# Top-4 routing of a mixture-of-experts layer: maxima marked by replacement, counts summed in PSUM, softplus by two subtractions

## The chip, the cores and the metric

One core of a Trainium2 chip runs the whole program. The metric is the time of one execution on the device in microseconds, the median over the runs shown; lower is better.

## The reference

The input x is 16 batches of 128 rows of 256 numbers. Four layers follow each other, each on the layer norm of x and added back to it: a gated long convolution with a context, a feed-forward layer with low-rank experts (top 2 of 16, softmax of the two), a quantized cross attention of 16 heads, and a feed-forward layer with 32 experts. The change sits in the routing of the last one, with two instructions in that of the second. Cut to it:

```python
logits = flat @ router_w.T                       # 2048 tokens x 32 experts
scores = jnp.sqrt(jax.nn.softplus(logits))
_, idx = jax.lax.top_k(scores + expert_bias, 4)
topv = jnp.take_along_axis(scores, idx, axis=1)
topv = topv / (topv.sum(axis=-1, keepdims=True) + 1e-20)
```

Each token's row then goes through its four experts (two products with a clamped gate, one back) and the results are summed with the weights topv; a shared expert takes all tokens.

## The kernel before

Each engine runs one program, written as a loop over ticks; a table per engine (T_PE, T_DVE, T_ACT, T_POOL, T_SP) says at which tick a step is written out for the first time, and most steps recur every 128 ticks, once per batch. The tables set nothing but the order of the instructions in each engine's queue; each queue is worked off in order, and semaphores tie the queues together. So at any time the steps of the convolution of one batch, the second layer of an earlier one and the attention of one before that are interleaved. From tick LOOP on the expert loop runs: 95 tiles of 128 rows, each with a gather, two transposes (L364, L365), the gate and up product (L380), the clamp and product on VectorE (L695, L697, L702), tanh on ScalarE (L1135), a transpose (L370), the down product (L347) and an indirect store.

Names in the code: PE is TensorE, dve VectorE, act ScalarE, pool GpSimd, sp SyncE. The four PSUM banks `ps` are handed out round robin by `bk.take`; whoever takes a bank waits for the semaphore of its last reader.

Routing works on groups of batches: 0 to 2 have four batches (128 columns of logits side by side), 3 and 4 have two. Group g's steps are: ScalarE takes abs and exp(-|l|) (step "ra", L1291, L1293); VectorE adds 1 ("rb", L945); ScalarE takes Ln ("rc", L1297); VectorE corrects the rounding of 1 + e by multiplying with e/((1+e)-1), adds max(l, 0) ("rd", L949 to L966); ScalarE takes the square root ("re", L1301); VectorE refines the root by one step, adds the bias, takes MAX8 and the maxima's indices ("top", L970 to L989); it builds the 0/1 mask of the four best by comparing a row of expert numbers with each index ("mb", L996 to L1003); PE multiplies the mask with a strict triangle (a token's place among its batch's tokens of this expert, L569) and with ones (the batch's count, L570), "rk"; VectorE adds the counts batch after batch into `cum`, adds place, count and the expert's base address, masks it and takes the four addresses with MAX8 ("cum", L1011 to L1026). GpSimd then scatters the token rows to these addresses in HBM (L1395). Each table load of ScalarE (ACT_TABLE_LOAD) appears under the line that needs it. After group 3 a table of tiles is computed from `cum` (L1028 and on), after group 4 the rest of it (L1030).

Steps that share queues with routing and that the prediction speaks of: L1213 copies the transposed, weighted low-rank values to SBUF, and PE's L469 multiplies with them; L1256 are the four exponentials of a head group, L900 its maxima, L1248 the copy behind which PE's L590 waits; L658 to L664 quantize, and PE's L493 and L514 transpose what they give; L856 adds the second layer's result, L653 and L655 take the statistics for the next norm, which GpSimd finishes (L1311 to L1315); L529 transposes the last norm's rows and takes the bank behind the counts; L839 computes 1 + or - tanh for the first router's two weights.

## Time and profile before

| | |
|---|---|
| median of 3 runs | 732.0 us (728.5 to 733.68) |
| the profiled execution | 729.9 us, its span 728.1 us |
| PE busy | 598.3 us, 82%, 4047 instructions |
| VectorE busy | 483.3 us, 66%, 1497 instructions |
| ScalarE busy | 379.2 us, 52%, 1106 instructions |
| GpSimd busy | 376.2 us, 52%, 526 instructions |
| granted TensorE clock, mean | 0.917 |

Busy time is the sum of an engine's instructions; the rest of the span it waits. The clock is given as a share of 2.4 GHz; 0.5 is the lower of its two levels. In lists in order of time a bracket behind an instruction gives the idle time of its engine just before it and the instruction that ended it.

### The profile page before, as it was taken

The page shows a single profiled execution, that of the slowest core. Times are in us where ns is not written, and L with a number is a line of the kernel's source. Part 1 is how long each engine was busy: PE and PEld are TensorE (multiplying, and loading weights), DVE is VectorE, ACT ScalarE, POOL GpSimd, SP SyncE. Part 2 cuts the span into 40 slices and gives each one's busy share as a digit, 9 for nine tenths or more (in the row PEclk, how much of TensorE's full clock was granted, in tenths as well). Part 3 has the DMA queues.
Part 4 walks back from the last instruction along what each step waited for, and adds up shares of the span by engine and source line. Part 5 has one row for each costly group of instructions (what it writes and reads, how often), then busy time and mean ns, then how long its engine had stood idle before and what let it go on. Part 6 is the DMA issues. An engine that isn't in the chain of part 4 may idle for free.

```text
span 728.1 us, 14326 instructions
## 1 busy us (share of the span) xinstructions
PE 598.3 (82%) x4047; PEld 478.0 (66%) x4047; DVE 483.3 (66%) x1497; ACT 379.2 (52%) x1106; POOL 376.2 (52%) x526
## 2 busy tenths in 40 slices
PE   1588899999988899978998897766777999999930
PEld 1477787777876787766876575543556877777810
DVE  1646757867888577767565774483754777655587
ACT  1002556666766367736466945551533666566620
POOL 6767846473563465775434235232163555555560
PEclk9999999999999899989996878895799999999985
DMA  7989999999999962132237925763343555455689
GB/s 275 221 245 335 335 335 334 333 319 324 312 325 312 322 213 84 46 111 75 83 101 266 372 60 161 265 200 114 100 131 95 161 161 155 147 161 158 193 277 302
DMA packets 135740, 155.02 MB, mean 213 GB/s; under 512 B 15248, under 2 KB 124944, under 8 KB 135408
## 3 DMA queue, kind: packets, MB, share of 16 engines
q1 hardware_dynamic: 117536, 122.50, 56.0%
q0 software_dynamic: 7632, 20.98, 8.1%
q10 hardware_dynamic: 10496, 10.62, 4.6%
q8 instruction: 36, 0.59, 0.3%
q14 instruction: 40, 0.33, 0.2%
HBM read 53.92 MB, written 100.28 MB: 212 GB/s over the span
## 4 chain that ended last, share of the span: by engine, by line
PE 61%; DVE 18%; issue 6%; POOL 6%; ACT 4%; DMA 3%; another core or an unknown queue 2%; ACTq 0%; SPq 0%; DVEq 0%; POOLq 0%
PE pc L639 10%; PE ps L380 10%; PE pS L347 6%; PE pS L619 4%; POOL arena L1381 3%; PE ps L605 3%; PE ps L425 2%; DMA work<-y_rows 2%; PE po L590 2%; PE ps L478 2%; PE ps L555 2%; PE ps L465 2%; PE ps L452 2%; PE ps L469 2%
## 5 line engine op out<-in xcount | busy, mean ns | idle before, releaser
L639 PE MATMUL pc<-arena,tk 128*128 128x128 f32 x768 | 112.9, 302 | 14.0 <-POOL arena L1381 7.3
L639 PEld LDWEIGHTS pc<-arena,tk 128*128 128x128 f32 x768 | 101.1, 209 | 27.0 <-issue 14.6
L380 PE MATMUL ps<-arena,work 128*128 x380 | 102.5, 394 | 2.3 <-ACT work L1145 2.3
L1381 POOL TENSOR_TENSOR arena<-arena 128x512 f32<-128x512 f32 x64 | 90.3, 1428 | 18.2 <-ACT arena L1191 18.0
L1395 POOL DMA_INDIRECT expert_rows<-stage,ixl x64 | 63.7, 995 | 44.4 <-DVE ixl L1026 26.0
L1256 ACT ACTIVATE work<-pS,work 128x128 f32<-128x128 f32 x256 | 72.8, 371 | 13.0 <-DVE work L900 11.4
L380 PEld LDWEIGHTS ps<-arena,work 128*128 128x128 f32 x380 | 67.1, 197 | 8.7 <-issue 2.9
L695 DVE TENSOR_SCALAR work<-ps 128x256 f32<-128x256 f32 x95 | 40.1, 422 | 49.1 <-PE ps L380 44.3
L347 PE MATMUL pS<-arena,tk 128*128 x190 | 60.6, 401 | 9.5 <-ACT tk L1140 8.7
L900 DVE TENSOR_REDUCE work<-pS 128x4 f32<-128x512 f32 x64 | 43.8, 684 | 30.9 <-PE pS L619 30.9
L1135 ACT ACTIVATE tk<-work 128x128 f32<-128x128 f32 x95 | 29.4, 310 | 58.9 <-DVE work L695 54.2
L882 DVE TENSOR_TENSOR arena<-pc,arena 128x512 f32<-128x512 f32 x64 | 43.4, 678 | 23.0 <-PE pc L639 23.0
L1323 POOL DMA_INDIRECT y_rows<-tk,work x38 | 41.5, 1093 | 29.0 <-ACT tk L1150 25.1
L347 PEld LDWEIGHTS pS<-arena,tk 128*128 128x128 f32 x190 | 28.6, 189 | 27.6 <-issue 19.3
L1311 POOL TENSOR_TENSOR stD<-stD,epsc 128x1 f32<-128x1 f32 x16 | 3.0, 190 | 84.4 <-DVE stD L655 84.4
L605 PE MATMUL ps<-pk,work 128*128 128x128 f32 x256 | 41.2, 286 | 5.6 <-ACT work L1241 2.9
L1248 ACT ACTIVATE work<-ps 128x512 f32<-128x512 f32 x64 | 37.8, 590 | 5.2 <-remote 2.2
L619 PE MATMUL pS<-arena,work 32*128 32x256 f32 x256 | 39.1, 425 | 0.2 <-ACT work L1241 0.2
L605 PEld LDWEIGHTS ps<-pk,work 128*128 128x128 f32 x256 | 31.3, 147 | 9.1 <-ACT work L1241 3.2
L1311 POOL TENSOR_TENSOR stB<-stB,epsc 128x1 f32<-128x1 f32 x16 | 3.1, 191 | 60.2 <-DVE stB L655 60.2
L425 PE MATMUL ps<-pk,arena 128*128 128x128 f32 x256 | 33.2, 277 | 0.0
L1140 ACT ACTIVATE tk<-po 128x128 f32<-128x128 f32 x95 | 26.1, 275 | 13.4 <-PE po L370 4.4
(288 smaller groups left out, 1484.2 us busy)
## 6 DMA issues: line engine op xcount, KB each, us to landing
expert_rows<-stage SPq DMA_DIRECT2D x32, 2080.0 KB, 21.5
work<-expert_rows SPq DMA_DIRECT2D x95, 130.0 KB
arena<-in_w SPq DMA_DIRECT2D x8, 1536.0 KB
stage<-xn_rows SPq DMA_DIRECT2D x64, 130.0 KB, 2.1
xn_rows<-xnD ACTq DMA_DIRECT2D x16, 512.0 KB
work<-y_rows SPq DMA_DIRECT2D x16, 512.0 KB, 5.7
tk<-in_tk SPq DMA_DIRECT2D x1, 2048.0 KB, 9.8
out<-xs SPq DMA_DIRECT2D x16, 128.0 KB, 2.7
```

What stands on the lines that cost most here:

```text
L347: i = pe.matmul(p[U * k:U * k + U, 0:256], hT[n % 2][:, U * k:U * k + U], arena[:, 512:][:, bass.ds(e, 256)], start=True, stop=True)
L380: i = pe.matmul(p[U * k:U * k + U, 0:256], xgT[n % 3][:, 128 * c + U * k:128 * c + U * k + U], arena[:, 256 * c:][:, bass.ds(e, 256)], sta ...
L425: i = pe.matmul(pv, zv[:, k, :], ident, is_transpose=True, start=False, stop=(k == 7))
L605: i = pe.transpose(p[:, 128 * k:128 * k + 128], Pt[m % 3][:, 128 * k:128 * k + 128], ident)
L619: i = pe.matmul(p[:, 256 * c:256 * c + 256], qT[b % 3][r, 128 * c:128 * c + 128], kz[b % 3][r, c, :, :].rearrange("p a b -> p (a b)"), sta ...
L639: i = pe.matmul(pv, tk[:, h, 128 * d:128 * d + 128], kvv[:, ci, :, :].rearrange("p b (i h j) -> p (b i) h j", i=8, h=8)[:, :, hl, :], star ...
L882: dve.tensor_tensor(zv, cbanks.place["conv", n][:, :].rearrange("p (k h j) -> p k h j", h=4, j=8), x1, ALU.mult).then_inc(s_z, 1)
L900: dve.tensor_reduce(mx[:, g, :], sbanks.place["S", m][:, :].rearrange("p (k m) -> p k m", k=4), AX.X, ALU.max, negate=True).then_inc(s_mx, 1)
L1256: i = act.activation(Pt[m % 3][:, 128 * k:128 * k + 128], sbanks.place["S", m][:, 128 * k:128 * k + 128], ACT.Exp, bias=mx[:, g, k:k + 1])
L1323: pool.indirect_dma_start(out=Yr, out_offset=bass.IndirectOffsetOnAxis(ap=xg[n % NX][:, 256:257].bitcast(U32), axis=0), in_=y[n % NY], in_ ...
L1381: pool.tensor_tensor(kv[kk % 4][:, c, half, :].rearrange("p (i h j) -> p i h j", h=8, i=8), i0, i1, ALU.mult).then_inc(s_kv, 1)
L1395: pool.indirect_dma_start(out=Xs, out_offset=bass.IndirectOffsetOnAxis(ap=ixl[:, b, k:k + 1], axis=0), in_=stage[:, j % NS, :], in_offset= ...
```

## The change

Softplus: ScalarE computes max(l, 0), 1 + e and Ln(1 + e) in one go (a step "ra" of five activations with a table load; "rb" and "rc" are gone), and VectorE forms A = max(Ln - (((1+e) - 1) - e), 1e-30) + max(l, 0). Mask: the bias is added into `score`, whose row has four columns of a very low value behind the 32; the four best values are copied into `m4`, filled up with that low value, match_replace writes `rest` with them replaced, and the mask is where `score` and `rest` differ. Counts: PE adds the earlier batches' counts of a group into the later batches' columns and sums all of the group's in one block of 32 columns; `ckey` holds the running count plus the base address. The first router's 1 + or - tanh moves to ScalarE. Cut to what matters (12 leading blanks are left out):

```diff
@@ -51,7 +52,7 @@
 LATER = {("top", 0): 45, ("top", 1): 45, ("mb", 0): 75, ("mb", 1): 75, ("rk", 0): 101, ("rk", 1): 101,
          ("cum", 0): 105, ("cum", 1): 105, ("list", 0): 136, ("list", 1): -78,
          ("list", 2): -170, ("st", 2): -110, ("list", 3): -182, ("st", 3): -117}
-LAST = {"ra": 1, "rb": 2, "rc": 3, "rd": 4, "re": 12, "top": 21, "mb": 31, "rk": 41, "cum": 42, "list": 52, "st": 0}
+LAST = {"ra": 1, "rd": 4, "re": 12, "top": 21, "mb": 31, "rk": 41, "cum": 42, "list": 52, "st": 0}
 STRIDE = (18, 24, 8, 8, 10)
 RG = 4
 SD = 32
@@ -566,8 +568,12 @@
         p, free = bk.take(("rk", g), s_cum, g + 1)
         pe.wait_ge(*free)
         pe.wait_ge(s_mb, g + 1)
-        pe.matmul(p[:, 0:w], bef[:, :], mb[:, 0:w], start=True, stop=True)
-        pe.matmul(p[:, 128:128 + w], oneb[:, :], mb[:, 0:w], start=True, stop=True).then_inc(s_rk, 1)
+        pe.matmul(p[:, 0:w], bef[:, :], mb[:, 0:w], start=True, stop=False)
+        for o in range(NE, w, NE):
+            pe.matmul(p[:, o:w], oneb[:, :], mb[:, 0:w - o], start=False, stop=(o + NE == w))
+        for o in range(0, w, NE):
+            i = pe.matmul(p[:, 128:128 + NE], oneb[:, :], mb[:, o:o + NE], start=(o == 0), stop=(o + NE == w))
+        i.then_inc(s_rk, 1)
     for m in (*at(t, T_PE["tabE"], 1, 2), *(2 + m for m in at(t, T_PE["tab"], 1, 2))):
         w = 4 * (NWE, NWL)[m // 2]
         p, free = bk.take(("regs", m), s_regs, m + 1)
@@ -836,8 +842,6 @@
         L, top, e2, s, co, c2 = (lv[:, 0:16], lv[:, 16:24], lv[:, 24:28], lv[:, 28:32], lv[:, 32:48],
                                  lv[:, 48:80].rearrange("p (k e) -> p k e", k=2))
         dve.wait_ge(s_e2, 2 * b + 2)
-        dve.scalar_tensor_tensor(out=s[:, 0:2], in0=R("pm"), scalar=e2[:, 1:2], in1=ones[:, 0:2],
-                                 op0=ALU.mult, op1=ALU.add).then_inc(*own.up())
         dve.wait_ge(*own.now())
         dve.tensor_tensor(c2, c2, s[:, 0:2].unsqueeze(2).broadcast_to((128, 2, 16)), ALU.mult)\
             .then_inc(*own.up())
@@ -939,31 +943,16 @@
         w = NE * (b1 - b0)
         return b0, b1, b1 - b0, tuple(rt[:, n, 0:w] for n in range(4))
 
-    for g in (g for g in range(NG) for _ in at(t, when(T_DVE, "rb", g), 1, 1)):
+    for g in (g for g in range(NG) for _ in at(t, when(T_DVE, "rd", g), 1, 1)):
         b0, b1, nb, (S_, A_, B_, C_) = group(g)
         dve.wait_ge(s_ra, g + 1)
-        dve.tensor_scalar(B_, A_, 1.0, None, ALU.add).then_inc(s_rb, 1)
-    for g in (g for g in range(NG) for _ in at(t, when(T_DVE, "rd", g), 1, 1)):
-        b0, b1, nb, (S_, A_, B_, C_) = group(g)
-        dve.wait_ge(s_rc, g + 1)
-        dve.tensor_scalar(B_, B_, -1.0, None, ALU.add).then_inc(*own.up())
-        dve.wait_ge(*own.now())
-        dve.tensor_scalar(S_, B_, 0.0, None, ALU.is_equal).then_inc(*own.up())
-        dve.tensor_scalar(B_, B_, 1e-30, None, ALU.max).then_inc(*own.up())
-        dve.wait_ge(*own.now())
-        dve.reciprocal(B_, B_).then_inc(*own.up())
-        dve.wait_ge(*own.now())
-        dve.tensor_tensor(C_, C_, B_, ALU.mult).then_inc(*own.up())
-        dve.wait_ge(*own.now())
-        dve.tensor_tensor(C_, C_, S_, ALU.add).then_inc(*own.up())
-        dve.wait_ge(*own.now())
-        dve.tensor_tensor(C_, C_, A_, ALU.mult).then_inc(*own.up())
-        dve.wait_ge(*own.now())
-        L = lg4[:, b0:b1, :].rearrange("p b e -> p (b e)")
-        dve.scalar_tensor_tensor(out=A_, in0=L, scalar=0.0, in1=C_, op0=ALU.max, op1=ALU.add)\
+        dve.scalar_tensor_tensor(out=B_, in0=B_, scalar=-1.0, in1=A_, op0=ALU.add, op1=ALU.subtract)\
             .then_inc(*own.up())
         dve.wait_ge(*own.now())
-        dve.tensor_scalar(A_, A_, 1e-30, None, ALU.max).then_inc(s_rd, 1)
+        dve.tensor_tensor(C_, C_, B_, ALU.subtract).then_inc(*own.up())
+        dve.wait_ge(*own.now())
+        dve.scalar_tensor_tensor(out=A_, in0=C_, scalar=1e-30, in1=S_, op0=ALU.max, op1=ALU.add)\
+            .then_inc(s_rd, 1)
     for g in (g for g in range(NG) for _ in at(t, when(T_DVE, "top", g), 1, 1)):
         b0, b1, nb, (S_, A_, B_, C_) = group(g)
         dve.wait_ge(s_re, g + 1)
@@ -973,51 +962,38 @@
         dve.wait_ge(*own.now())
         dve.tensor_tensor(S_, B_, S_, ALU.add).then_inc(*own.up())
         dve.wait_ge(*own.now())
-        dve.tensor_scalar(S_, S_, 0.5, None, ALU.mult).then_inc(*own.up())
-        dve.wait_ge(*own.now())
-        dve.tensor_tensor(v3(C_), v3(S_), R("eb").unsqueeze(1).broadcast_to((128, nb, NE)),
-                          ALU.add).then_inc(*own.up())
+        if g == 0:
+            dve.wait_ge(s_pconst, 2)
+        dve.scalar_tensor_tensor(out=score[:, 0:nb, 0:NE], in0=v3(S_), scalar=0.5,
+                                 in1=R("eb").unsqueeze(1).broadcast_to((128, nb, NE)), op0=ALU.mult,
+                                 op1=ALU.add).then_inc(*own.up())
         dve.wait_ge(*own.now())
         for b in range(nb):
-            i = dve.max(m8[:, b, :], v3(C_)[:, b, :])
+            i = dve.max(m8[:, b, :], score[:, b, 0:NE])
         i.then_inc(*own.up())
         dve.wait_ge(*own.now())
-        for b in range(nb):
-            i = dve.max_index(i8[:, b, :], m8[:, b, :], v3(C_)[:, b, :])
-        i.then_inc(*own.up())
-        dve.wait_ge(*own.now())
-        dve.tensor_copy(f8[:, 0:nb, :], i8[:, 0:nb, :]).then_inc(*own.up())
+        dve.tensor_copy(m4[:, 0:nb, 0:KT], m8[:, 0:nb, 0:KT]).then_inc(*own.up())
         dve.wait_ge(*own.now())
     for g in (g for g in range(NG) for _ in at(t, when(T_DVE, "mb", g), 1, 1)):
         b0, b1, nb, (S_, A_, B_, C_) = group(g)
-        io = R("iota")[:, 0:NE].unsqueeze(1).broadcast_to((128, nb, NE))
-        for k in range(KT):
-            o = A_ if k == 0 else B_
-            dve.tensor_tensor(v3(o), io, f8[:, 0:nb, k:k + 1].broadcast_to((128, nb, NE)), ALU.is_equal)\
-                .then_inc(*own.up())
-            dve.wait_ge(*own.now())
-            if k:
-                dve.tensor_tensor(A_, A_, B_, ALU.add).then_inc(*own.up())
-                dve.wait_ge(*own.now())
-        dve.tensor_copy(mb[:, 0:NE * nb], A_).then_inc(s_mb, 1)
-        dve.tensor_tensor(Sall[:, b0:b1, :], v3(A_), v3(S_), ALU.mult).then_inc(*own.up())
+        for b in range(nb):
+            i = dve.match_replace(rest[:, b, :], m4[:, b, :], score[:, b, :], GONE)
+        i.then_inc(*own.up())
+        dve.wait_ge(*own.now())
+        dve.tensor_tensor(v3(mb[:, 0:NE * nb]), score[:, 0:nb, 0:NE], rest[:, 0:nb, 0:NE],
+                          ALU.not_equal).then_inc(s_mb, 1)
+        dve.wait_ge(s_mb, g + 1)
+        dve.tensor_tensor(Sall[:, b0:b1, :], v3(mb[:, 0:NE * nb]), v3(S_), ALU.mult)
     for g in (g for g in range(NG) for _ in at(t, when(T_DVE, "cum", g), 1, 1)):
         b0, b1, nb, (S_, A_, B_, C_) = group(g)
         p = place["rk", g]
+        last = R("key") if g == 0 else ckey[:, g - 1, :]
         dve.wait_ge(s_rk, g + 1)
-        if g == 0:
-            dve.wait_ge(s_pconst, 2)
-        for b in range(nb):
-            dve.tensor_tensor(cum[:, b0 + b + 1, :], p[:, 128 + NE * b:128 + NE * b + NE],
-                              cum[:, b0 + b, :], ALU.add).then_inc(*own.up())
-            dve.wait_ge(*own.now())
-        dve.tensor_tensor(v3(B_), p[:, 0:NE * nb].rearrange("p (b e) -> p b e", e=NE), cum[:, b0:b1, :],
-                          ALU.add).then_inc(s_cum, 1)
-        dve.wait_ge(s_cum, g + 1)
-        dve.tensor_tensor(v3(B_), v3(B_), R("key")[:, 0:NE].unsqueeze(1).broadcast_to((128, nb, NE)),
+        dve.tensor_tensor(v3(B_), v3(p[:, 0:NE * nb]), last.unsqueeze(1).broadcast_to((128, nb, NE)),
                           ALU.add).then_inc(*own.up())
-        dve.wait_ge(*own.now())
-        dve.tensor_tensor(Ball[:, b0:b1, :], v3(B_), v3(A_), ALU.mult).then_inc(*own.up())
+        dve.tensor_tensor(ckey[:, g, :], p[:, 128:128 + NE], last, ALU.add).then_inc(s_cum, 1)
+        dve.wait_ge(*own.now())
+        dve.tensor_tensor(Ball[:, b0:b1, :], v3(B_), v3(mb[:, 0:NE * nb]), ALU.mult).then_inc(*own.up())
         dve.wait_ge(*own.now())
         for b in range(b0, b1):
             i = dve.max(key[:, b, :], Ball[:, b, :])
@@ -1025,9 +1001,15 @@
         dve.wait_ge(*own.now())
         dve.tensor_scalar(ixl[:, b0:b1, :], key[:, b0:b1, 0:KT], -1.0, None, ALU.add).then_inc(s_ixl, 1)
     for _ in at(t, T_DVE["eta"], 1, 1):
-        floor_of(cum[:, GROUPS[3][1], :], tiles_[:, 1, :], tiles_[:, 0, :], 1.0 / U, 0.5 * (U - 1) / U)
+        dve.wait_ge(s_cum, 4)
+        dve.tensor_tensor(tiles_[:, 1, :], ckey[:, 3, :], R("key"), ALU.subtract).then_inc(*own.up())
+        dve.wait_ge(*own.now())
+        floor_of(tiles_[:, 1, :], tiles_[:, 1, :], tiles_[:, 0, :], 1.0 / U, 0.5 * (U - 1) / U)
     for _ in at(t, T_DVE["ta"], 1, 1):
-        floor_of(cum[:, NB, :], tiles_[:, 1, :], tiles_[:, 0, :], 1.0 / U, -0.5 * (U - 1) / U)
+        dve.wait_ge(s_cum, 5)
+        dve.tensor_tensor(tiles_[:, 1, :], ckey[:, 4, :], R("key"), ALU.subtract).then_inc(*own.up())
+        dve.wait_ge(*own.now())
+        floor_of(tiles_[:, 1, :], tiles_[:, 1, :], tiles_[:, 0, :], 1.0 / U, -0.5 * (U - 1) / U)
         dve.tensor_tensor(tiles_[:, 1, :], tiles_[:, 1, :], taken[:, :], ALU.subtract).then_inc(*own.up())
     for _ in (*at(t, T_DVE["eta"], 1, 1), *at(t, T_DVE["ta"], 1, 1)):
         scan_step(tiles_[:, 1, :], scan[:, 0, :], 1)
@@ -1203,9 +1185,11 @@
         act.activation(hb[0][:, 1, :], place["h", b][0:64, 0:128], ACT.Tanh, bias=hrb1[:, :],
                        scale=0.5).then_inc(s_eh, 1)
     for b in at(t, T_ACT["e2"], 128, NB):
-        e2 = lg[b % 2][:, 24:28]
+        e2, s = lg[b % 2][:, 24:28], lg[b % 2][:, 28:32]
         act.wait_ge(s_e2, 2 * b + 1)
-        act.activation(e2[:, 1:2], e2[:, 0:1], ACT.Tanh, scale=0.5).then_inc(s_e2, 1)
+        act.activation(e2[:, 1:2], e2[:, 0:1], ACT.Tanh, scale=0.5).then_inc(*own.up())
+        act.wait_ge(*own.now())
+        act.activation(s[:, 0:2], R("pm"), ACT.Copy, bias=1.0, scale=e2[:, 1:2]).then_inc(s_e2, 1)
     for b in at(t, T_ACT["wxT"], 128, NB):
         if b >= 2:
             act.wait_ge(s_wb, b - 1)
@@ -1288,13 +1272,15 @@
         act.wait_ge(s_lg4, b1)
         if g:
             act.wait_ge(s_ixl, g)
+        w = NE * (b1 - b0)
         act.activation(A_, L, ACT.Abs).then_inc(*own.up())
+        act.activation(rt[:, 0, 0:w], L, ACT.Relu)
         act.wait_ge(*own.now())
-        act.activation(A_, A_, ACT.Exp, scale=-1.0).then_inc(s_ra, 1)
-    for g in (g for g in range(NG) for _ in at(t, when(T_ACT, "rc", g), 1, 1)):
-        w = NE * (GROUPS[g][1] - GROUPS[g][0])
-        act.wait_ge(s_rb, g + 1)
-        act.activation(rt[:, 3, 0:w], rt[:, 2, 0:w], ACT.Ln).then_inc(s_rc, 1)
+        act.activation(A_, A_, ACT.Exp, scale=-1.0).then_inc(*own.up())
+        act.wait_ge(*own.now())
+        act.activation(rt[:, 2, 0:w], A_, ACT.Copy, bias=1.0).then_inc(*own.up())
+        act.wait_ge(*own.now())
+        act.activation(rt[:, 3, 0:w], rt[:, 2, 0:w], ACT.Ln).then_inc(s_ra, 1)
     for g in (g for g in range(NG) for _ in at(t, when(T_ACT, "re", g), 1, 1)):
         w = NE * (GROUPS[g][1] - GROUPS[g][0])
         act.wait_ge(s_rd, g + 1)
```

The tables of ticks lose "rb" and "rc"; all else keeps its tick. The instructions move at these places. ScalarE in group 0's batch, before; lg is the logits, rt the routing tiles, L1213 the copy for PE's L469:

```order
L1208 ACTIVATE lg<-lg 128x1
L1256 ACTIVATE work<-pS,work 128x128 x4
L1291 ACTIVATE rt<-lg 128x128
L1293 ACTIVATE rt<-rt 128x128
L1213 ACTIVATE work<-ps 128x256
L1297 ACT_TABLE_LOAD
L1297 ACTIVATE rt<-rt 128x128
L1248 ACTIVATE work<-ps 128x512
```

and now (line numbers are those of the changed kernel; L1197 is the same copy, L1232 the former L1248):

```order
L1190 ACTIVATE lg<-lg 128x1
L1192 ACTIVATE lg<-rows,lg 128x2
L1240 ACTIVATE work<-pS,work 128x128 x4
L1276 ACTIVATE rt<-lg 128x128
L1277 ACTIVATE rt<-lg 128x128
L1279 ACTIVATE rt<-rt 128x128
L1281 ACTIVATE rt<-rt 128x128
L1283 ACT_TABLE_LOAD
L1283 ACTIVATE rt<-rt 128x128
L1197 ACTIVATE work<-ps 128x256
L1232 ACTIVATE work<-ps 128x512
```

The table load and Ln moved ahead of the copy, and two activations came in before them. There are 20 table loads in either program. VectorE behind group 0's maxima, before; f is the indices, mb the mask:

```order
L996 TENSOR_TENSOR rt<-rows,f 128x128 x2
L1000 TENSOR_TENSOR rt<-rt 128x128
L996 TENSOR_TENSOR rt<-rows,f 128x128
L1000 TENSOR_TENSOR rt<-rt 128x128
L996 TENSOR_TENSOR rt<-rows,f 128x128
L1000 TENSOR_TENSOR rt<-rt 128x128
L1002 CAST mb<-rt 128x128
L1003 TENSOR_TENSOR Sall<-rt 128x128
L870 TENSOR_TENSOR work<-ps,rows 128x16x16
```

and now:

```order
L980 MATCH_REPLACE rest<-m,score 128x36 x4
L983 TENSOR_TENSOR mb<-score,rest 128x128
L986 TENSOR_TENSOR Sall<-mb,rt 128x128
L874 TENSOR_TENSOR work<-ps,rows 128x16x16
L904 TENSOR_REDUCE work<-pS 128x4
```

Nine instructions became six, with the same neighbours. PE at group 0's counts, now (before, one product with `bef` and one with `oneb`, 128x128 each, stood in this place):

```order
L480 MATMUL ps<-arena,pk 128x128 x4
L571 MATMUL ps<-mb,bef 128x128
L573 MATMUL ps<-mb,oneb 128x96
L573 MATMUL ps<-mb,oneb 128x64
L573 MATMUL ps<-mb,oneb 128x32
L575 MATMUL ps<-mb,oneb 128x32 x4
L611 MATMUL ps<-pk,work 128x128 x4
```

Six products came in ahead of L611, the former L605.

## Rows read from the trace of the kernel before

**Rows 1.** Busy time by stretch; start:end, length, busy us (instructions) by engine, clock, DMA.

```profile
214.00:240.00 26.00, 19.72 (x143) 14.75 (x142) 22.27 (x73) 13.34 (x35) 10.00 (x20) 0.91 1.00 319
510.00:530.00 20.00, 15.70 (x59) 10.73 (x58) 16.03 (x78) 10.37 (x28) 3.95 (x4) 0.78 0.36 98
560.00:600.00 40.00, 39.78 (x215) 31.66 (x214) 29.75 (x107) 25.80 (x96) 22.31 (x24) 1.00 0.52 153
```

**Rows 2.** Page, part 4: shares of the chain that ended last, by engine.

```profile
PE 61%; DVE 18%; issue 6%; POOL 6%; ACT 4%; DMA 3%; another core or an unknown queue 2%; ACTq 0%; SPq 0%; DVEq 0%; POOLq 0%
```

**Rows 3.** PE in order of time: start, length, instruction, [idle before <- releaser].

```profile
227.91 0.30 PE L493 MATMUL ps<-pk,work 128*128 128x128 f32 x1 [1.34 <-DVE work L664]
...
336.01 0.30 PE L493 MATMUL ps<-pk,work 128*128 128x128 f32 x1 [2.21 <-DVE work L664]
```

**Rows 4.** The same view: PE at the bank wait of groups 0 and 1.

```profile
239.91 0.47 PE L529 MATMUL ps<-pk,xnD 128*128 128x128 f32 x1 [2.97 <-DVE rt L1014]
...
347.33 0.33 PE L529 MATMUL ps<-pk,xnD 128*128 128x128 f32 x1 [1.78 <-DVE rt L1014]
```

**Rows 5.** VectorE by line: names, shapes, count | busy us, mean ns | idle before.

```profile
L839 DVE SCALAR_TENSOR_TENSOR lg<-rows,lg,ones 128x2 f32<-128x2 f32 x16 | 6.9, 433 | 6.7 <-ACT lg L1208 6.6
...
L996 DVE TENSOR_TENSOR rt<-rows,f 128x128 f32<-128x128 f32 (+1 forms) x20 | 6.2, 309 | 0.5
...
L954 DVE RECIPROCAL rt<-rt 128x128 f32<-128x128 f32 (+1 forms) x5 | 4.0, 793 | 0.2
...
L986 DVE FIND_INDEX8 i<-m,rt 128x8 uint32<-128x32 f32 x16 | 2.7, 184 | 0.0
...
L986 DVE MATCH_VALUE_LOAD i<-m,rt 128x8 f32 x16 | 1.2, 78 | 0.2
```

**Rows 6.** Order of time around group 1's softplus: VectorE, GpSimd, PE.

```profile
295.96 0.23 DVE L949 TENSOR_SCALAR rt<-rt 128x128 f32<-128x128 f32 x1
...
299.05 0.42 DVE L856 TENSOR_TENSOR xs<-ps,xs 128x256 f32<-128x256 f32 x1
...
300.23 0.19 POOL L1311 TENSOR_TENSOR stC<-stC,epsc 128x1 f32<-128x1 f32 x1 [2.99 <-DVE stC L655]
...
318.39 0.45 PE L529 MATMUL ps<-pk,xnD 128*128 128x128 f32 x1 [4.00 <-ACT xnD L1128]
```

**Rows 7.** Order of time, group 0's burst behind the maxima: VectorE and GpSimd.

```profile
222.02 0.61 DVE L996 TENSOR_TENSOR rt<-rows,f 128x128 f32<-128x128 f32 x2
...
223.32 0.82 DVE L1000 TENSOR_TENSOR rt<-rt 128x128 f32<-128x128 f32 x1
...
225.65 0.42 DVE L870 TENSOR_TENSOR work<-ps,rows 128x256 f32<-128x256 f32 x1
...
223.05 0.95 POOL L1355 TENSOR_TENSOR arena<-arena 128x256 f32<-128x256 f32 x1
```

**Rows 8.** Instructions of one tile, the counts' second product: ns min/median/max.

```profile
L570 PE MATMUL ps<-mb,oneb x5: 193/219/219, 233.8 to 522.2; 128*128 128x128 bf16 x3, 128*128 128x64 bf16 x2
```

**Rows 9.** Order of time around group 0's Ln: ScalarE, then PE.

```profile
190.35 0.37 ACT L1213 ACTIVATE work<-ps 128x256 f32<-128x256 f32 x1
190.73 1.28 ACT L1297 ACT_TABLE_LOAD   x1
192.03 0.31 ACT L1297 ACTIVATE rt<-rt 128x128 f32<-128x128 f32 x1
...
191.36 1.03 PE L469 MATMUL ps<-pk,work 128*128 128x256 f32 x4
192.87 0.43 PE L590 MATMUL po<-work 128*32 128x128 f32 x8 [0.49 <-ACT work L1248]
```

**Rows 10.** Order of time, VectorE: the last group's first and last step.

```profile
512.68 0.20 DVE L949 TENSOR_SCALAR rt<-rt 128x64 f32<-128x64 f32 x1 [1.37 <-ACT rt L1297]
...
524.40 0.17 DVE L1026 TENSOR_SCALAR ixl<-key 128x8 uint32<-128x8 f32 x1
```

**Rows 11.** Order of time, VectorE: a wait for something unknown ("remote").

```profile
549.53 0.43 DVE L919 TENSOR_SCALAR tk<-ps 128x256 f32<-128x256 f32 x1 [4.63 <-remote]
```

21 lines of the change are left out of this document (12 added, 9 removed).

## The prediction

> **What bounds the kernel now.** I read four views in this order: the busy time by stretch, PE's list in order of time with its waits, the groups of instructions by line, and the chain of waits. The stretches show three kinds of time [rows 1]. From 560 to 600 us the expert loop keeps PE busy for 39.78 of 40.00 us at granted clock 1.00, so nothing that leaves VectorE can shorten it. Around the first group's routing (214 to 240 us) PE is busy for only 19.72 of 26.00 us, at clock 0.91, while VectorE is busy for 22.27: here VectorE is late. From 510 to 530 PE idles 4.3 us at clock 0.78 with the last group's routing in between. The whole chain is 61% PE and 18% VectorE [rows 2]. So a VectorE saving is worth something only where PE waits for the queue in which routing sits: 1.34 us in group 0 and 2.21 us in group 1 before the transposes of line 493 [rows 3], and 2.97 and 1.78 us before line 529, which waits for the PSUM bank that the routing counts hold [rows 4]. Group 2's batch shows no such wait of over 0.4 us.
>
> **The change, part by part.** *Softplus.* VectorE's ten steps (line 945 and lines 949 to 966) become three. In group 1 lines 949 to 966 run from 295.96 to 299.05, 3.1 us [rows 6]; three steps of 0.33 us (line 996's 309 ns [rows 5] and the gap behind it) make 1.0, so 2.1 us go; the reciprocal alone is 793 ns. In group 1 these steps stand ahead of the statistics for which GpSimd waits 2.99 us; GpSimd then works on in its order, and PE waits 4.00 us for what comes out of it by way of ScalarE [rows 6]. The line between (856) needs PE's line 469 too, so of 2.1 us I count 1.6. In group 0 the same saving goes nowhere: VectorE next waits for PE's scores.
>
> *Top four.* FIND_INDEX8 with its MATCH_VALUE_LOAD (184 + 78 ns [rows 5]) goes 16 times and match_replace comes 16 times. The trace of before has no match_replace. Its nearest row is that pair, which I take (0.26 us); the upper end is two two-input steps (0.6 us), 16 x 0.35 = 5.5 us more in all; a gain below the pair is excluded, as the instruction reads more columns (36 against 32) and writes them. The comparisons, additions and the cast (20 + 15 + 5 instructions) become one comparison per group. In group 0 the burst that ended with the product ran from 222.02 to 225.65, 3.63 us [rows 7]; four match_replace, the comparison and the product now make 1.05 + 0.33 + 0.33 = 1.7, so 1.9 go. The burst before it loses the index pairs (1.05) and one fused step (0.33), 1.4. So VectorE is 3.3 us earlier at the quantize steps on which line 493 waits. PE idles 26.00 - 19.72 = 6.28 us in this stretch, 2.97 of them the bank wait; of the other 3.3 I count 3.0. In group 1 I count the whole wait, 2.2.
>
> *The shared port.* Line 1000's step takes 0.82 us instead of 0.29 in the same burst, while a GpSimd multiplication with two inputs runs (223.05 to 224.00) [rows 7]; it is one of the removed ones, and its excess of 0.5 us is inside the 3.63. The Trainium skill ("SBUF — State Buffer", Who interferes with whom) says that a VectorE instruction with two SBUF inputs blocks against a GpSimd instruction that reads SBUF, and one with a single input outside the two-port modes does not. The row agrees for the two-input side, and nothing here shows the other. By that rule match_replace never stalls; without it a burst would save up to 0.5 us less. The sum does not use it.
>
> *Counts.* PE gets three more products with shifted columns and three more with 32 in a group of four. Such a product takes at most 0.19 to 0.22 us by itself [rows 8], and its neighbours overlap: between 6 x 0.05 and 6 x 0.2 us; I take 0.3 for a big group and 0.1 for a small one, 1.1 in all. Other PE work is queued behind, so it counts in full. In return the bank is free after two VectorE reads instead of five: at 0.2 us for a 32-column step (as the FIND_INDEX8 of rows 5) that is 0.6 us earlier at each of the two bank waits, 1.3 with the shorter gaps.
>
> *Softmax of the first router.* Line 839 (433 ns mean, 16 times [rows 5]) moves to ScalarE, behind a wait for its own tanh; queued behind it there are the four exponentials. VectorE loses 6.9 us, but for most of that it then waits for PE; ScalarE gets 16 x 0.4 (a step of 0.31 as in rows 9, and the wait). I count a gain of 1.0, with bounds of -6.4 (all of ScalarE's share on the path) and 3 (half of VectorE's).
>
> *ScalarE's order.* The table load and Ln, which stood behind the copy of line 1213, now stand ahead of it, behind two added steps (0.31 us each as the Ln of rows 9). In group 0 the copy began at 190.35; with two steps (overlapping, 0.55), the load (1.28) and Ln (0.31) ahead of it, it begins at 192.5 and ends at 192.9. PE's line 469 needs the copy and began at 191.36; it will begin at about 193.0. PE waited 0.49 us anyway at 192.87 [rows 9], so the loss is about 1.0 us, and the same in group 1. In group 2 PE comes later than the copy. The loss is 2.0, between 0.9 (only the added steps) and 3.5. In the trace Ln starts 0.02 us behind the end of the table load (190.73 + 1.28 to 192.03) [rows 9]. The Trainium skill ("ScalarE: Activation LUTs", What ACT_TABLE_LOAD costs) adds a drain of some 1.38 us to each load. The trace disagrees, and the measurement decides; by the page the copy would be later by as much again and the two losses 2.8 us larger.
>
> *Last two groups.* In the last, VectorE's routing runs from 512.68 to 524.57 with the first tiles of the expert loop in its gaps [rows 10]. Its steps have half the columns, 0.26 us with the gap by my estimate from the mixed 309 ns; softplus loses six steps, the maximum's burst three, the comparisons five, the counts two: 16 x 0.26 = 4.1 us, and ScalarE gets 0.4 more. The tiles pass through PE at a lower clock in this time and PE's idle time is 4.3 us, so I count 2.0. The group before it, with the same instructions, sits between the last two batches: 2.0. Group 2 gets 0.9, for two waits of under 0.4 us.
>
> *Clock.* The granted clock of 0.91 over 26 us is 2.3 us of lost PE work around group 0 [rows 1], in a stretch where the full level gives way behind PE's waits. The bank wait stays for the most part, so I count 1.2 here and 1.0 in group 1: 2.2.
>
> The gains are 1.6 + 3.0 + 2.2 + 1.3 + 1.0 + 4.0 + 0.9 + 2.2 = 16.2 us, the costs 1.1 + 2.0 = 3.1; 13.1 remain at the places. Between them other queues set the pace: GpSimd's row scatters, and waits of several engines for something unknown (4.63 us at 549.53 [rows 11]). By the chain's shares [rows 2] at most 61 + 18 + 4% of the span passes a shift on; with the GpSimd-bound stretch behind group 1 I take 0.65, between 0.4 and 0.85. That gives 8.5 us. Against the profiled execution's 729.9 us this is 721.4. The median of the runs, 732.0, is 2.1 above it; by it the same gain gives 723.5. I forecast 722.
>
> **The rivals.** *(a) Absorbed.* PE works in order, and the saving on VectorE turns into waits for GpSimd or for PE itself: 35% is passed on and the costs are at their upper ends, 16.2 x 0.35 - 4.5 = 1.2 us, so 730. For it speaks that VectorE is only 18% of the chain; against it the waits of rows 3, which name VectorE. *(b) All comes through,* and the clock stays up at the bursts: 13.1 + 2 = 15 us, so 716. The 22.27 busy us of VectorE in 26 speak for it, the bank wait against it. *(c) ScalarE becomes the link: slower.* What routing adds to ScalarE stands ahead of the exponentials and of the copy that PE waits for: 16 x 0.4 and 3 x 1.5 = 11 us, less the 2 of the last group: 739 to 741. It decides from the point where PE waits over 0.4 us for ScalarE in every batch; now there are 0.49 at one place of a routing batch [rows 9]. ScalarE's 13.34 busy us of 26.00 [rows 1] speak against it. *(d) match_replace is dear:* 5.5 us more, a third of them on the path: 724. *(e)* The waits for something unknown come and go with the programs' lengths, by up to 4.6 us either way; this widens every case.
>
> **How the numbers follow.** Forecast (717 to 727, with (d) in it) 0.46, (a) 0.27, (b) 0.19, (c) 0.08. A measurement of this kernel tells about 1%, 7.3 us, from no change: below 724.7 is faster, above 739.3 slower. Faster: 0.19 from (b), 0.36 from the forecast, 0.03 from (a) by (e), 0.58. Slower: 0.07, nearly all from (c). The rest is the same, 0.35. The range takes in (b) and most of (a), 712 to 732; about 0.1 lies above it and 0.08 below.
>
> **What would show it.** Right: the waits before line 493 (1.34 and 2.21) vanish, the bank waits shrink by 0.6 each, the burst of 3.63 us measures 1.4 to 1.8, and VectorE's busy time falls by about 35 us in all (softplus 11, comparisons 12, line 839 7, counts 4, the fused step 1); line 469 in groups 0 and 1 starts late behind a wait for ScalarE. Wrong: if VectorE's busy time falls so and PE's idle time from 214 to 240 does not, (a) holds; if PE's waits for ScalarE grow by over 5 us in sum, (c); if a match_replace takes over 0.5 us, (d).

## The result, and the profile after

The changed kernel took 707.8 us in the median of 4 runs (702.2 to 710.6), the kernel before 732.5 beside it (4 runs): ratio 0.966, 95% interval 0.962 to 0.971, so 24.8 us less. The forecast was 722, a gain of 10. The profiled run after took 710.6 us (span 708.7), the one before 729.9 (span 728.1); the two traces therefore account for 19.4 of the 24.8 us. The runs were taken in six sets, each with runs of the kernel before beside it, and that kernel stood at 728 to 733 us in three of the sets and at 701 to 703 in the other three (on one chip, number 10, at both), so only ratios and differences within a set are compared, and the ratios leave out the executions that fell in a slower state.

Part 1 and the head of part 4 of the page after (the chain before is [rows 2]):

```profile
PE 585.5 (83%) x4069; PEld 470.2 (66%) x4069; DVE 456.7 (64%) x1392; ACT 384.8 (54%) x1132; POOL 375.4 (53%) x527
...
PE 61%; DVE 15%; issue 8%; POOL 6%; ACT 5%; DMA 3%; another core or an unknown queue 2%; ACTq 0%; SPq 0%; DVEq 0%; POOLq 0%
```

VectorE was busy for 483.3 us before and is for 456.7 now. That is 26.6 us less, not the 35 of the forecast. The lines that the change touches did lose about 34 (softplus 11, mask 12, line 839 7, counts 4), but other steps of VectorE took longer, such as this one of the first router, the second behind the step that moved:

```profile
L845 DVE TENSOR_TENSOR lg<-lg 128x16 f32<-128x16 f32 x16 | 6.4, 397 | 0.5
...
L849 DVE TENSOR_TENSOR lg<-lg 128x16 f32<-128x16 f32 x16 | 8.7, 546 | 0.5
```

The first surprise is PE: 598.3 us busy before, 585.5 now, though it got 22 more products. Busy time times mean granted clock is nearly the same, 598.3 x 0.917 = 548.6 and 585.5 x 0.938 = 549.2, and it lies between 546.6 and 550.4 in all eighteen traces without filler products. So the 12.8 us go with the clock. PE's idle time fell by the other 6.6 of the 19.4 us. Busy time by stretch shows where, with the copy of PE's attention output (line 1263 before, 1247 after) as the milestone of each batch. Before, for the batches around the bursts of group 0, group 1 (two batches) and group 2:

```profile
223.90:255.80 31.90, 26.62 (x187) 21.21 (x186) 21.49 (x64) 14.95 (x42) 11.37 (x22) 0.84 1.01 321
...
302.30:332.20 29.90, 24.60 (x186) 20.46 (x186) 20.56 (x63) 16.59 (x44) 22.85 (x30) 0.89 0.26 81
332.20:361.90 29.70, 25.28 (x188) 20.85 (x188) 19.12 (x61) 13.89 (x40) 14.95 (x23) 0.89 0.29 87
...
407.90:437.50 29.60, 26.14 (x165) 19.29 (x166) 23.92 (x86) 18.37 (x49) 9.41 (x15) 0.83 0.48 169
```

and between the same milestones after:

```profile
224.80:252.20 27.40, 24.20 (x194) 19.89 (x193) 18.61 (x55) 15.14 (x43) 11.23 (x21) 0.94 0.99 315
...
298.60:323.80 25.20, 21.91 (x186) 18.10 (x186) 22.41 (x58) 17.03 (x45) 20.77 (x26) 1.00 0.31 97
323.80:354.70 30.90, 26.66 (x197) 21.40 (x197) 18.14 (x53) 14.24 (x40) 15.20 (x24) 0.83 0.28 82
...
400.70:428.50 27.80, 23.00 (x171) 17.60 (x172) 19.68 (x74) 18.64 (x51) 8.74 (x14) 0.94 0.51 177
```

Group 0's stretch is 4.5 us shorter, 2.4 of them PE's busy time, at clock 0.94 instead of 0.84. Group 1 gains 4.7 in its first batch and gives back 1.2 in the second, where the clock stands lower than before. Such a step back in one batch is within what one program does: in two traces of the changed kernel at the other level (changed_again and changed_third, below) this batch took 28.7 and 25.9 us, at clock 0.88 and 1.00. From 214 to 240 us, where the prediction read 6.28 us of idle time of PE, 3.32 are left.

PE in order of time, the waits of [rows 3, 4] and the last one of [rows 6] as they are now:

```profile
227.13 0.30 PE L495 MATMUL ps<-pk,work 128*128 128x128 f32 x1 [0.77 <-DVE work L670]
...
237.33 0.33 PE L531 MATMUL ps<-pk,xnD 128*128 128x128 f32 x1 [2.00 <-DVE ckey L994]
...
312.61 0.30 PE L531 MATMUL ps<-pk,xnD 128*128 128x128 f32 x1 [1.25 <-ACT xnD L1110]
...
326.05 0.30 PE L495 MATMUL ps<-pk,work 128*128 128x128 f32 x1 [0.66 <-DVE work L670]
...
339.22 0.48 PE L531 MATMUL ps<-pk,xnD 128*128 128x128 f32 x1 [1.88 <-DVE ckey L994]
```

And VectorE's burst of group 0, the answer to [rows 7]:

```profile
223.01 0.08 DVE L980 MATCH_VALUE_LOAD rest<-m,score 128x8 f32 x1
223.08 0.18 DVE L980 MATCH_REPLACE8 rest<-m,score 128x36 f32<-128x36 f32 x1
223.18 0.08 DVE L980 MATCH_VALUE_LOAD rest<-m,score 128x8 f32 x1
...
223.79 0.29 DVE L983 TENSOR_TENSOR mb<-score,rest 128x128 bf16<-128x128 f32 x1
224.11 0.83 DVE L986 TENSOR_TENSOR Sall<-mb,rt 128x128 f32<-128x128 bf16 x1
224.87 0.41 DVE L874 TENSOR_TENSOR work<-ps,rows 128x256 f32<-128x256 f32 x1
```

From the first match_replace to the step behind the burst it is 224.87 - 223.01 = 1.86 us, where it was 3.63. One pair starts 0.17 us behind the other (the load overlaps the search before it).

### The profile page after: what moved, and what is told of

The parts are those of the page before. It is cut to its first block, busy times and chain, and to the rows that moved or that the text cites. A ratio compares the mean times of both kernels' runs of the same rounds, so it can differ in the third digit from the quotient of the medians.

```text
span 708.7 us, 14308 instructions
## 1 busy us (share of the span) xinstructions
PE 585.5 (83%) x4069; PEld 470.2 (66%) x4069; DVE 456.7 (64%) x1392; ACT 384.8 (54%) x1132; POOL 375.4 (53%) x527
## 4 chain that ended last, share of the span: by engine, by line
PE 61%; DVE 15%; issue 8%; POOL 6%; ACT 5%; DMA 3%; another core or an unknown queue 2%; ACTq 0%; SPq 0%; DVEq 0%; POOLq 0%
PE pc L645 10%; PE ps L382 10%; PE pS L349 5%; PE pS L625 4%; POOL arena L1368 4%; PE ps L427 3%; PE ps L611 3%; PE po L596 2%; DMA work<-y_rows 2%; PE ps L557 2%; PE ps L480 2%; PE ps L471 2%; PE ps L454 2%; PE ps L467 2%
## 5 line engine op out<-in xcount | busy, mean ns | idle before, releaser
L645 PE MATMUL pc<-arena,tk 128*128 128x128 f32 x768 | 110.7, 298 | 13.3 <-POOL arena L1368 7.3
L645 PEld LDWEIGHTS pc<-arena,tk 128*128 128x128 f32 x768 | 98.9, 205 | 25.7 <-issue 13.7
L382 PE MATMUL ps<-arena,work 128*128 x380 | 99.0, 383 | 2.6 <-ACT work L1127 2.4
L382 PEld LDWEIGHTS ps<-arena,work 128*128 128x128 f32 x380 | 65.3, 192 | 8.6 <-issue 3.5
L886 DVE TENSOR_TENSOR arena<-pc,arena 128x512 f32<-128x512 f32 x64 | 43.5, 679 | 25.9 <-PE pc L645 25.9
L611 PE MATMUL ps<-pk,work 128*128 128x128 f32 x256 | 39.8, 279 | 3.8 <-ACT work L1240 1.6
L1232 ACT ACTIVATE work<-ps 128x512 f32<-128x512 f32 x64 | 37.8, 591 | 6.0 <-remote 3.2
L611 PEld LDWEIGHTS ps<-pk,work 128*128 128x128 f32 x256 | 30.5, 144 | 6.8 <-issue 2.4
L1122 ACT ACTIVATE tk<-po 128x128 f32<-128x128 f32 x95 | 25.8, 272 | 13.1 <-remote 6.8
```

Of the source, the lines that this page charges most:

```text
L382: i = pe.matmul(p[U * k:U * k + U, 0:256], xgT[n % 3][:, 128 * c + U * k:128 * c + U * k + U], arena[:, 256 * c:][:, bass.ds(e, 256)], sta ...
L611: i = pe.transpose(p[:, 128 * k:128 * k + 128], Pt[m % 3][:, 128 * k:128 * k + 128], ident)
L645: i = pe.matmul(pv, tk[:, h, 128 * d:128 * d + 128], kvv[:, ci, :, :].rearrange("p b (i h j) -> p (b i) h j", i=8, h=8)[:, :, hl, :], star ...
L886: dve.tensor_tensor(zv, cbanks.place["conv", n][:, :].rearrange("p (k h j) -> p k h j", h=4, j=8), x1, ALU.mult).then_inc(s_z, 1)
```

## The experiments

### One part alone

Four kernels, each the one before with one part of the diff:

```diff
-        Ball = sb("Ball", [128, NB, NE])
+        Ball = sb("Ball", [128, NB + 1, NE])
...
-        cum = sb("cum", [128, NB + 1, NE])
+        cum = Ball
```

The diff is what only_mask needs beside its hunks, since score and rest do not fit next to cum: the sums stand in the rows of Ball that are not written yet. whole_less_counts and the first combined kernel below do the same. only_softplus takes the hunks of lines 949 to 955 and 1277 to 1283 of the kernel after, only_counts the added products, ckey and the two reads of the bank, only_tanh_scale the hunk of line 839.

> The kernel before with the new top-four mask alone (match_replace, fused score step, one comparison; the counts' running sums live in the rows of Ball that are not written yet, the rest as before). Theory A (the granted clock): most of the 19.4 us between the two traces is work of PE that ran at 2.4 instead of 1.2 GHz (PE busy 598.3 -> 585.5 us although it got more instructions), so what shortens PE's waits inside a burst brings more than the wait: this part alone gives 9 to 14 us, 718 to 723, PE's busy time falls by 5 to 9 us, and the mean clock rises by about 0.01. Theory B (waits alone): a part is worth what PE's waits at the transposes behind the burst lose (1.3 + 2.2 and some 2 at the last group): 4 to 6 us, 726 to 728, PE's busy time within 2 us of 598.

> The kernel before with the new softplus alone (three VectorE steps, Relu, 1+e and Ln on ScalarE in one block). Theory A (clock): 3 to 6 us, with PE's busy time 2 to 4 us lower; the granted clock of 302 to 332 us, 0.89 before, goes to 1.00. Theory B (waits alone): PE's wait at the transposes of line 529 in group 1 (4.00 us) falls by 2, and ScalarE's order gives back 1 to 2: 730 to 733.

> The kernel before with the counts summed in PSUM alone (six products more in a group of four, two VectorE reads of the bank instead of five). Both theories: the waits for the bank (2.97 and 1.78 us) fall by 0.6 to 1 each, PE's products cost 0.3 each; A says 1 to 4 us faster, since these waits stand where the clock gives way in groups 0 and 1, B says 0 to 2.

> The kernel before with the first router's scaling step moved from VectorE to ScalarE alone. Until 198 us the trace after is 1.1 to 1.8 us behind the one before, so this part is worth nothing where the loads set the pace, and the 9 batches behind it have the ScalarE step on the path as much as the VectorE step was: -1 to +2 us, 730 to 733 by both theories. A third theory, that this part carries most of the 24.8 us as it is in every batch, would give 12 us or more, below 720.

Measured beside 29 runs of the kernel before (728.4): mask 713.9, ratio 0.981 (0.977 to 0.986), by the ratio 13.6 us less; softplus 728.7, 1.001 (0.998 to 1.005), 1 us more; counts 725.4, 0.997 (0.994 to 1.000), 2.2 less; the ScalarE step 724.9, 0.996 (0.992 to 0.999), 3.1 less. The mask lands at the upper end of theory A (9 to 14) and far beyond B's 4 to 6; PE's busy time is 587.2 us, 11 below the trace before, more than A's 5 to 9. The ScalarE step brought more than the 2 us that both theories allowed. Together the four fall short of 1 by 0.025, the whole change by 0.034 (0.030 to 0.038) in its own set. Softplus goes B's way. Its trace shows why in group 1, again between the milestones:

```profile
305.10:332.50 27.40, 23.52 (x186) 19.73 (x187) 22.35 (x63) 16.53 (x43) 20.60 (x26) 0.94 0.29 88
332.50:366.60 34.10, 28.35 (x191) 23.16 (x191) 20.88 (x62) 14.00 (x41) 15.64 (x25) 0.80 0.25 75
```

The first batch is 2.5 us shorter than before (29.90), the second 4.4 longer (29.70), with the old burst still in it and the clock at 0.80 (one trace each, and this batch varies as said above).

### The whole less one part, and the logarithm's place

Four kernels are the one after with one part as it was before. after_ln_behind_copy is the kernel after with

```diff
-                    act.activation(rt[:, 2, 0:w], A_, ACT.Copy, bias=1.0).then_inc(*own.up())
-                    act.wait_ge(*own.now())
-                    act.activation(rt[:, 3, 0:w], rt[:, 2, 0:w], ACT.Ln).then_inc(s_ra, 1)
+                    act.activation(rt[:, 2, 0:w], A_, ACT.Copy, bias=1.0).then_inc(s_ra, 1)
+                for g in (g for g in range(NG) for _ in at(t, when(T_ACT, "rc", g), 1, 1)):
+                    w = NE * (GROUPS[g][1] - GROUPS[g][0])
+                    act.wait_ge(s_ra, g + 1)
+                    act.activation(rt[:, 3, 0:w], rt[:, 2, 0:w], ACT.Ln).then_inc(s_rc, 1)
```

> The changed kernel with the old softplus. Alone the new softplus was worth nothing (ratio 1.0014): in its trace it was 2.5 us ahead at the first batch of group 1 and lost 4.4 at the second, where PE still waited 2.68 us for the burst and the clock fell to 0.80. If its gain was swallowed by the old burst (parts depend on each other), it comes out now: the kernel without it is 4 to 8 us slower than the whole change, about 2.3 to 2.8% faster than before (ratio 0.972 to 0.977). If the parts simply add, this kernel equals the whole change, ratio 0.966.

> The changed kernel with the logarithm and its table load behind the copy of line 1197 again, as they stood before. In the trace of the changed kernel that copy is 1.8, 0.9 and 1.9 us late in groups 0, 1 and 2 against its batch. By the prediction's term for ScalarE's order this gives back 2.0 us: ratio 0.963 to 0.964. The rival is that PE has slack there and waits elsewhere for it: no change, 0.966, since in groups 1 and 2 the whole lateness at the next batch's copy of line 1247 is 0.1 us or less.

> The changed kernel itself, on the same chip as the three below, since the chips differ (the kernel before had a median of 732.5, 728.4 and 701.4 us on the three used so far). Theory A (clock): the gain shrinks on a chip on which the clock of the kernel before falls less: ratio 0.966 where the mean clock of before is 0.92, 0.970 to 0.975 where it is 0.948. Theory B (waits alone): the same ratio, 0.966, on every chip.

> The changed kernel with the old top-four burst (indices, four comparisons, three additions, cast, product). If the parts add, it is 14 us (the mask's gain alone) slower than the changed kernel. If they depend on each other through the waits behind the burst, more: 17 to 22 us, so that softplus, counts and the ScalarE step together are worth 3 to 7 us without it.

> The changed kernel with the old running counts (two products, a VectorE addition for each batch out of the bank; the sums in the unwritten rows of Ball). Alone the new ones gained 2.2 us (0.997). Additive: 2 us slower than the changed kernel. With interplay (the bank wait is the longest that is left behind the burst, 2.00 and 1.88 us): 3 to 6 us.

> The changed kernel with the first router's scaling step back on VectorE. Alone the move gained 3 us (0.9958, 0.9921 to 0.9994). Additive: 3 us slower than the changed kernel. If the move only helps where VectorE is late because of the old burst: 0 to 1 us.

The first two ran in one set (before 701.4): 684.2 (0.975, 0.971 to 0.979) and 682.8 (0.973, 0.968 to 0.977). With the logarithm in its old place the new softplus is worth 1.4 us, inside the noise. The changed kernel wasn't in that set; its 0.977 and 0.976 in the two that followed would make the logarithm's place worth 2 to 3 us, but the intervals overlap, so that the order costs 2.0 is neither shown nor excluded. For the same reason the forecasts of both, which started from 0.966, decide nothing.

The other four ran in the next set (before 703.4). The changed kernel: 686.8, 0.977 (0.973 to 0.981), 16.6 us less. Without the mask 700.6, 0.996: the mask is worth 13.8 us, which is what adding parts says (14), not 17 to 22. Without the counts 682.2, 0.971 (0.966 to 0.975): 4.6 us *faster* than the whole, where both readings of its expectation had it 2 to 6 slower; the intervals of the two overlap a little. Without the ScalarE step 688.0, 0.977: no difference that can be told, where adding parts says 3. Leaving the mask out costs 0.019 of the time, as much as it gains alone. The two traces (11.2 us apart) don't show this group by group: the three batches at the bursts of groups 0 and 1 differ by 2.1 us, the two of group 2 by 7.3. Group 2's batch, without the mask and with it:

```profile
399.10:429.60 30.50, 25.07 (x171) 18.75 (x172) 22.63 (x83) 18.54 (x51) 7.73 (x13) 0.89 0.54 195
```

```profile
395.20:420.20 25.00, 21.62 (x171) 16.55 (x172) 19.69 (x74) 18.36 (x51) 8.47 (x13) 1.00 0.73 261
```

The first is of whole_less_mask, the second of changed_again: 5.5 us in one batch, 3.5 of them PE's busy time for as many instructions, at a clock of 0.89 instead of 1.00.

The expectations speak of chips; since chip 10 showed both levels, it is the set that counts. The ratio was to go with the clock of the kernel before, 0.970 to 0.975 where that is 0.948. It went that way and further, 0.977 at a mean clock of 0.943 against 0.966 in the first set; one ratio for all levels (theory B) is out.

### PE kept busy in its waits

before_filled is the kernel before with these products of constants (no part of the output); after_filled has the same ahead of its own waits, with other counts:

```diff
+                    for _ in range({7: 1, 11: 1}.get(b, 0)):
+                        pe.matmul(p[:, :], ident, P("A")[:, 0:512], start=True, stop=True)
                     pe.wait_ge(s_xi, b + 1)
...
+                    if b in {5: 3, 8: 3, 9: 2, 14: 2}:
+                        pe.wait_ge(*cbanks.free[0])
+                    for _ in range({5: 3, 8: 3, 9: 2, 14: 2}.get(b, 0)):
+                        pe.matmul(cbanks.tiles[0][:, :], ident, P("A")[:, 0:512], start=True, stop=True)
                     p, free = bk.take(("x4", b), s_x4, b + 1)
```

> The kernel before, in which PE fills its six longest waits of the routing batches with products of constants that nobody reads (12 of 512 columns, 0.45 us each at the full clock: 3, 3, 2, 2 before the transposes of line 529 of the batches 5, 8, 9, 14, one each before those of line 493 of the batches 7 and 11). It removes no wait and adds 5.6 us of PE work. Theory A (the clock falls because PE sits idle at the bursts): the granted clock of the stretches behind these waits (0.84, 0.89, 0.89, 0.81) rises, by 0.05 or more on the mean of these four, and the time falls by 2 to 8 us, or at least does not rise. Theory B (waits alone; the clock falls by itself): no gain in clock, and 0 to 4 us slower.

> The changed kernel with 9 such products in what is left of its waits (2, 1, 2 before the transposes of line 531 of the batches 5, 8, 9; one each before line 495 in 7 and 11; two before line 516 in batch 8). Theory A: 2 to 6 us faster than the changed kernel, ratio to before 0.958 to 0.964, mean clock 0.945 to 0.955 over the runs (median of four runs before: 0.942). Theory B: 0 to 3 us slower than the changed kernel, ratio 0.966 to 0.970.

before_filled took 697.7 us beside 701.4: 0.995 (0.992 to 0.998), 12 runs. It is faster though it only adds work. The median of the runs' mean clocks is 0.958, beside 0.948. PE in order of time at group 0's bank wait, and the stretches by the same milestones (groups 0, 1, 1 and the batches up to 400 us):

```profile
236.97 2.74 PE L531 MATMUL pc<-pk 128*128 128x512 f32 x6
240.13 0.33 PE L535 MATMUL ps<-pk,xnD 128*128 128x128 f32 x1 [0.42 <-DVE rt L1020]
```

```profile
224.90:253.40 28.50, 26.23 (x197) 19.63 (x196) 21.72 (x64) 15.05 (x43) 11.58 (x22) 1.00 0.98 316
301.00:328.90 27.90, 23.45 (x182) 17.99 (x181) 19.92 (x59) 15.09 (x39) 21.52 (x27) 1.00 0.28 87
328.90:356.00 27.10, 25.08 (x194) 19.26 (x194) 19.64 (x61) 13.97 (x41) 15.40 (x24) 1.00 0.32 95
356.00:400.00 44.00, 37.14 (x304) 28.65 (x304) 30.98 (x94) 33.16 (x91) 19.33 (x34) 1.00 0.61 210
```

(A product of 512 columns is two instructions: 3 of them, x6, take 2.74 us, 0.91 each. The twelve make 11 us of PE work, not the 5.6 that the expectation counted.) The granted clock is 1.00 in all four. The trace before has 0.84, 0.89 and 0.89 in the first three, but it is of the other level; the nearest trace at this level with the old burst and no fillers is whole_less_mask's, in the same stretches:

```profile
224.30:252.80 28.50, 24.19 (x193) 19.02 (x192) 20.27 (x59) 15.11 (x43) 11.42 (x22) 0.94 1.00 317
299.50:326.60 27.10, 23.52 (x186) 19.73 (x187) 21.79 (x62) 16.78 (x44) 20.61 (x26) 0.94 0.30 90
326.60:355.30 28.70, 23.78 (x193) 19.28 (x193) 19.49 (x56) 14.27 (x42) 15.42 (x24) 0.94 0.29 89
355.30:400.00 44.70, 39.11 (x297) 29.46 (x297) 27.43 (x81) 33.20 (x91) 20.20 (x34) 0.92 0.61 210
```

So with PE's idle time at the bursts filled, 2.4 GHz stay, and the runs' clock says the same. This much of theory A holds: idle time at the bursts costs twice, once as the wait and again as the half clock behind it. In the median 3.7 us are left after 11 us of added work. For the changed kernel no gain shows: after_filled took 686.1, 0.977 (0.972 to 0.982), clock 0.956, and the changed kernel has 0.977 and 0.976 in the next two sets; A's 0.958 to 0.964 is missed. Its trace has clock 1.00 in group 0's batch, but 0.94 in group 1's first in spite of the fillers, 0.78 to 0.94 in the four batches from 371 to 468 us, which have none, and 0.93 in the expert loop.

### Where the mask's time is passed on

Three kernels are the changed one with steps whose result is overwritten, four behind the copy to m4 and five ahead of the match_replace; in padded_late the groups are (2, 3, 4), in padded_group2 (2,), in padded_early

```diff
+                    for _ in range(4 if g in (0, 1) else 0):
+                        dve.tensor_tensor(rest[:, 0:nb, 0:NE], score[:, 0:nb, 0:NE], score[:, 0:nb, 0:NE],
+                                          ALU.add).then_inc(*own.up())
+                        dve.wait_ge(*own.now())
...
+                    for _ in range(5 if g in (0, 1) else 0):
```

> The changed kernel as the measure for the three below on their chip. If the chip's before has a median of some 702 us, ratio 0.973 to 0.980 as on the last one; if it has some 730, 0.963 to 0.970. A clock theory needs the two to go together; the theory of waits alone needs one ratio for both.

> The changed kernel with 4 steps (0.33 us each with the gap) behind the copy of the maxima and 5 ahead of the match_replace in groups 0 and 1 alone, as long as what the new mask took out there (1.4 and 1.8 us). The prediction gave the mask 5.2 us in these two groups and some 3 in the other three. By it this kernel is 5 us slower than the changed one. If the time that the mask gained lies behind group 1 (in the traces 7.3 of the 13.8 us appear in group 2's batches), 2 to 5 us here and 6 to 9 in the other one. If PE's waits are not the measure at all, no difference (within 2 us).

> The same steps in groups 2, 3 and 4 alone. By the prediction's terms 2 to 3 us slower than the changed kernel; by the traces 6 to 9. Both padded kernels together should come to the 13.8 us that the whole mask was worth on the last chip, if it is its length that counts; if they come to clearly less (under 7), the mask's gain is in the kind of its instructions (two-input steps that stop while GpSimd multiplies), not in their length.

> The steps of padded_late in group 2 alone. padded_late was 7.1 us slower than the changed kernel on its chip. By the prediction (0.9 for group 2, 4.0 for the last two) this one is 1 to 2 us slower than the changed kernel; if group 2's time is the term that was missed, 4 to 6 us (ratio to before 0.981 to 0.984 where the changed kernel has 0.9756); if it is the last two groups, 0 to 1.5.

In one set (before 702.3): changed kernel 684.5, 0.976 (0.972 to 0.979); padded_early 691.2, 0.986 (0.982 to 0.989); padded_late 692.4, 0.986 (0.983 to 0.989). So 6.7 and 7.9 us more. What the padding adds to VectorE is read from order of time; the steps of group 0 in padded_early:

```profile
218.87 1.27 DVE L978 TENSOR_TENSOR rest<-score 128x128 f32<-128x128 f32 x4
...
224.49 2.12 DVE L984 TENSOR_TENSOR rest<-score 128x128 f32<-128x128 f32 x5
```

The two bursts of a group, from their first to their last step, grow in padded_early by 1.31 + 1.63 us (group 0) and 1.04 + 1.67 (group 1), 5.7 in sum, and the kernel by 6.7. In padded_late by 3.8, 2.5 and 2.3, 8.6 in sum, and the kernel by 7.9. Together 14.2 us of VectorE time cost 14.6, each of the two differences good to about 2.5 us: in sum, what a burst grows by is passed on. The same measure of the mask: its two bursts shrank, between the traces before and after, by 2.7, 2.5, 3.5, 2.3 and 1.9 us in the five groups, 12.9 in all, and it is worth 13.8 or 13.6. Whether it is the length of the steps or their kind (two inputs, held up while GpSimd multiplies) the padding can't fully tell, since its steps have two inputs too. But in padded_early one of the nine steps of a group was held (five took 2.12 us, where four took 1.27), in place of the product for Sall that is held in the changed kernel, and the kernel still lost 6.7 us for 5.7; that speaks for the length. Part of the length is the holding up itself: seven steps of 0.63 to 0.91 us stand in the old bursts behind the maxima (0.20 to 0.31 elsewhere), two of 0.83 in the new ones.

padded_group2 ran in another set (before 730.9), where the changed kernel did not: 714.6, 0.978 (0.973 to 0.983). Against the changed kernel's 0.976 it is 1.5 us slower, as the prediction's terms say, against its 0.966 at this level 8 us, so it decides nothing. The milestones of padded_late's trace against changed_third's put 3.8 us into group 2's batch, one execution each.

### A combined kernel

combined_old_counts is the kernel after with the logarithm behind the copy and the old counts, and with the product for Sall behind the maxima of the keys; combined_new_counts is the same with the new counts.

```diff
-                    dve.wait_ge(s_mb, g + 1)
-                    dve.tensor_tensor(Sall[:, b0:b1, :], v3(mb[:, 0:NE * nb]), v3(S_), ALU.mult)
...
+                    dve.wait_ge(s_mb, g + 1)
+                    dve.tensor_tensor(Sall[:, b0:b1, :], v3(mb[:, 0:NE * nb]), v3(S_), ALU.mult).then_inc(*own.up())
+                    dve.wait_ge(*own.now())
                     dve.tensor_scalar(ixl[:, b0:b1, :], key[:, b0:b1, 0:KT], -1.0, None, ALU.add).then_inc(s_ixl, 1)
```

> An attempt to beat both: mask, softplus and ScalarE step of the change, the logarithm behind the copy, the old running counts (whole_less_counts was 4.6 us faster than the changed kernel), and the product for Sall (0.83 us in the burst of group 0, stopped by GpSimd) moved behind the keys. Expected 4 to 8 us faster than the changed kernel on this chip. If the 4.6 us were chance, 1 to 3.

> The combined kernel with the change's counts in PSUM instead of the old running ones. If the new counts cost 4.6 us, as whole_less_counts says, it is 3 to 6 us slower than the combined kernel with the old ones: ratio 0.972 to 0.976. If the gain of the combined kernel comes from the two moves (logarithm, product for Sall), it equals it: 0.965 to 0.970.

combined_old_counts: 678.0 us (5 runs), 0.967 (0.964 to 0.971), 24.3 less than before and 6.5 less than the changed kernel of the same set: it beats both. Which of its three differences (logarithm, counts, product for Sall) brings how much was not taken apart. combined_new_counts ran in the last set: 710.9 beside 730.9, 0.972 (0.967 to 0.978). That lies in the range for counts that cost 3 to 6 us, but its interval reaches into the other range (0.965 to 0.970), and the two combined kernels ran at different levels, between which the changed kernel itself moved by 0.01. So the cost of the new counts rests on whole_less_counts alone, and how it comes about isn't shown. The bank waits of changed_again, then the second one in changed_third (the same program), then both of whole_less_counts:

```profile
237.29 0.33 PE L531 MATMUL ps<-pk,xnD 128*128 128x128 f32 x1 [2.00 <-DVE ckey L994]
...
337.47 0.48 PE L531 MATMUL ps<-pk,xnD 128*128 128x128 f32 x1 [2.25 <-DVE ckey L994]
```

```profile
337.80 0.33 PE L531 MATMUL ps<-pk,xnD 128*128 128x128 f32 x1 [2.26 <-DVE ckey L994]
```

```profile
237.41 0.48 PE L531 MATMUL ps<-pk,xnD 128*128 128x128 f32 x1 [2.98 <-DVE rt L993]
...
337.14 0.33 PE L531 MATMUL ps<-pk,xnD 128*128 128x128 f32 x1 [1.78 <-DVE rt L993]
```

The wait is 1.0 us shorter with the new counts in group 0 and 0.5 longer in group 1. The half clock behind it (transposes of 0.48 us instead of 0.33) comes with either kind of counts: in group 1 of changed_again but not of changed_third, and in group 0 of whole_less_counts. The runs' mean clock is 0.949 with the new counts and 0.958 without. Why six small products should push it down was not tried, and stays open.

## Why the prediction was wrong

The direction was right, and so was the place in groups 0 and 1; the size was not. Two steps failed, the share of 0.65 and the terms of groups 2 to 4, and a third, the clock's 2.2, was too small for the set that it was meant for. In the order of its steps:

- **"I take 0.65" (the share passed on).** The prediction applied one share, read from the chain, to every term. The runs show two kinds of VectorE time. In the bursts of the mask the share is about 1: 12.9 us shorter bursts brought 13.8 and 13.6, 14.2 us of padding cost 14.6. The other parts pass on little: softplus runs 2.2 us shorter in each of three groups and 1.6 in two (9.9 us in sum) and brought nothing alone and 1.4, inside the noise, in company; the ScalarE step takes 7 us off VectorE and is worth 3.1 us in one set and 1.2 in another. This alone does not explain the miss: with a share of 1 the prediction's 13.1 us give 719, still inside its range.
- **Softplus, 1.6.** The time that VectorE saves here turns into waits. In group 1 VectorE finished the three steps and then waited for PE, which had waited 0.30 us for ScalarE's late copy:

```profile
292.06 0.29 DVE L954 SCALAR_TENSOR_TENSOR rt<-rt 128x128 f32<-128x128 f32 x1
292.94 0.42 DVE L860 TENSOR_TENSOR xs<-ps,xs 128x256 f32<-128x256 f32 x1 [0.59 <-PE ps L471]
```

  In groups 2 and 4 it waited 1.59 and 3.95 us for ScalarE's logarithm before the first of the three steps.

- **Top four, 3.0 and 2.2.** The length is confirmed: the burst came down from 3.63 to 1.86 us (1.7 forecast), and rival (d) is out. But the pair was misread. 0.26 us is the sum of the two instructions, which overlap; the index pairs of before already started 0.16 to 0.18 us apart:

```profile
216.79 0.19 DVE L986 FIND_INDEX8 i<-m,rt 128x8 uint32<-128x32 f32 x1
...
216.95 0.18 DVE L986 FIND_INDEX8 i<-m,rt 128x8 uint32<-128x32 f32 x1
```

  Four took 0.74 us, not 1.05, so the burst of the maxima lost 0.95 us and not 1.4, and four match_replace take 0.75. The waits before the transposes did not vanish, 0.77 and 0.66 us are left, and one of 0.43 stands behind each (line 516; before there was none in group 0 and 0.42 in group 1).
- **The shared port.** The two-input product in the same burst was held to 0.83 us, while GpSimd multiplied; this agrees with the Trainium skill ("SBUF — State Buffer", Who interferes with whom), which says so of two inputs and the opposite of one. All 16 MATCH_REPLACE8, with one input, took 178 to 182 ns. In the traces of the changed kernel they ran beside GpSimd steps of 128x1 only; in padded_early four of them ran beside a large one with two inputs, just as fast:

```profile
226.73 0.18 DVE L988 MATCH_REPLACE8 rest<-m,score 128x36 f32<-128x36 f32 x1
...
226.54 0.73 POOL L1354 TENSOR_TENSOR arena<-arena,rows 128x256 f32<-128x256 f32 x1
```

  So the rule holds on both sides here. Of the two steps that were held in group 0, line 1000's 0.82 us and the one behind it,

```profile
224.18 0.77 DVE L996 TENSOR_TENSOR rt<-rows,f 128x128 f32<-128x128 f32 x1
```

  one is left, line 986's.
- **Bank waits, 0.6 each.** In group 0 2.97 became 2.00; in group 1 1.78 became 1.88. The counts as a whole, forecast at 1.3 less 1.1, gave 2.2 us alone (an interval that touches no change) and cost 4.6 in the whole: the sign is not the same.
- **ScalarE's order, 2.0.** The mechanism is in the trace, word for word in group 0:

```profile
191.69 1.28 ACT L1283 ACT_TABLE_LOAD   x1
192.98 0.31 ACT L1283 ACTIVATE rt<-rt 128x128 f32<-128x128 f32 x1
193.20 0.36 ACT L1197 ACTIVATE work<-ps 128x256 f32<-128x256 f32 x1
...
193.62 1.13 PE L471 MATMUL ps<-pk,work 128*128 128x256 f32 x4 [1.05 <-ACT work L1197]
```

  PE waits 1.05 us there (0.30 in group 1) for the copy. The next ACTIVATE again starts 0.01 us behind the load's end, so no drain shows in this trace either. Between the milestones of group 0 only 0.7 us are lost (the trace after lags by 1.06 us at the batch before and by 1.80 at this one), and the move of the logarithm alone was not resolved. So no run shows the 2.0.
- **Group 2, 0.9, and the last two, 4.0.** This is the second step that failed. The three groups were sized by what PE was seen to wait, 4.9 us for all parts; there the mask's bursts alone shrank by 3.5 + 2.3 + 1.9 = 7.7 us, and padded_late, 8.6 us of VectorE time in groups 2 to 4, cost 7.9. (In the sum for the last groups softplus loses seven steps, not six; that is 0.26 us.) Group 2 was judged by its waits of under 0.4 us, but its batch took 5.5 us more with the old mask in one pair of traces, 3.5 of them as a lower clock. A batch in which no single wait is long can still be set by VectorE. With a share of 1, and 7.7 for 4.9, the prediction's sum is 15.9 us, near the 16.6 and 17.8 of the later sets.
- **Clock, 2.2.** Too small for the set that the forecast was for: between its two traces PE's busy time fell by 12.8 us. At the other level it is less. Take PE's work as 549 us over the mean clock, an estimate from the products above: in the changed kernel's second set (0.943 before, 0.949 after) the clock makes 3.7 of the 16.6 us, and against 0.942 without the mask it makes 4.3 of the mask's 13.8. The rest is idle time of PE that went.
- **Rivals.** (b), all comes through, 716, was the nearest, and still 8 us short in the first set. (a) is out by its own sign: PE's idle time from 214 to 240 us fell from 6.28 to 3.32. (c) is out too: PE's waits for ScalarE sum to some 45 us before and 46 after, not 5 more. (e) was wrong in its reason: see below.

What stays open is why the first set gave 0.966 (up to 0.971) and the later two 0.977 and 0.976 (from 0.973 and 0.972 up). The 8 us between them are about what the clock brought more in the first set (12.8 against 3.7), but why it does at this level isn't shown; combined_new_counts, at the same level, has 0.972, and the changed kernel ran there only four times.

## What to carry to other kernels

Don't spread one pass-through over a change: ask of each removed step what its engine waits for next. Where the engine goes straight on to work that others wait for, a microsecond was worth about a microsecond here; where it ran into a wait for PE or ScalarE, next to nothing. On a kernel that lives near the clock's edge, compare PE's busy time before and after for the same instructions: its fall is a term of the sum. Do it within one set of runs and over more than one trace, since the clock of a single batch varies from 0.88 to 1.00 in the same program. And measure the parts of a change alone and by leaving them out: here one part carried the gain, and one that seemed to gain 2 us alone (0.994 to 1.000) cost 4.6 in company.

## What the runs showed that was not expected

**The unknown waits belong to the set of runs, not to the program.** All eight traces of the three sets at 728 to 733 us have waits "remote" of ScalarE and VectorE, 10 to 28 us of them on VectorE; none of the twelve traces of the sets at 701 to 703 has one. The same copy in the trace after and in changed_third, the same program:

```profile
483.78 0.60 ACT L1247 ACTIVATE work<-po 128x512 f32<-128x512 f32 x1 [5.92 <-remote]
```

```profile
465.97 0.60 ACT L1247 ACTIVATE work<-po 128x512 f32<-128x512 f32 x1 [2.42 <-PE po L596]
```

Part 4 of the page of changed_third, which names no unknown queue at all:

```profile
PE 67%; DVE 15%; issue 5%; ACT 5%; POOL 4%; DMA 3%; ACTq 0%; SPq 0%; DVEq 0%; POOLq 0%
```

Chip 10 showed both levels in two sets, 28.6 us apart for the kernel before. What is on the other end was not found, nor whether these waits make the level; the gap is larger than the change itself, and only comparisons inside a set are safe from it.

**Useless work can pay.** Twelve products of 512 columns that nobody reads made the kernel before 3.7 us faster (ratio 0.992 to 0.998). Its trace keeps the granted clock at 1.00 through groups 0 and 1, and the runs' mean clock rose from 0.948 to 0.958.
